# Turning half of a softmax tile through memory and VectorE squares instead of on TensorE, for three of sixteen attention units per image

## The reference

```python
# layer 0: group norm, 8 heads of 64 channels, projection, group norm, residual
hn = group_norm(x, gn1_scale, gn1_bias)
q, k, v = split(einsum('bchw,oc->bohw', hn, w_qkv) + b_qkv)      # per head, 64 x 1024 each
wgt = softmax(einsum('bct,bcs->bts', q * scale, k * scale))      # per head, 1024 x 1024
a = einsum('bts,bcs->bct', wgt, v)
x = x + group_norm(einsum('bchw,oc->bohw', a, w_proj) + b_proj, gn2_scale, gn2_bias)
# layer 1: one head of 512 channels, weights normalised, rms over q, k and v
scores = einsum('bci,bcj->bij', q1, k1) * 512 ** -0.5
h = einsum('oc,bcn->bon', w_out, einsum('bij,bcj->bci', softmax(scores), v1))
out = (x + h) * 2 ** -0.5
```

## Time and profile before

| | |
|---|---|
| median of 3 runs | 3375.08 us (3374.36 to 3375.76) |
| the profiled execution, its own time | 3375.88 us |
| its span, first to last instruction | 3373.7 us |
| TensorE busy | 3351.2 us, 99% |
| VectorE busy | 2132.7 us, 63% |
| ScalarE busy | 1838.7 us, 55% |
| GpSimd busy | 1064.3 us, 32% |
| granted TensorE clock | 1.00 of 2.4 GHz |
| DMA, mean | 98 GB/s |

### The profile page before, as it was taken

One profiled execution on the slowest core, in us unless ns is written; L12 is line 12 of the kernel. 1 busy time (PEld: TensorE's weight loads), 2 busy tenths in 40 slices (PEclk: granted clock), 3 DMA queues, 4 the chain that ended last, 5 costly groups with the idle time before them and its releaser, 6 DMA issues.

```text
span 3373.7 us, 51950 instructions
## 1 busy us (share of the span) xinstructions
PE 3351.2 (99%) x16816; PEld 2777.5 (82%) x16816; DVE 2132.7 (63%) x3489; ACT 1838.7 (55%) x3094; POOL 1064.3 (32%) x947
## 2 busy tenths in 40 slices
PE   8999999999999999999999999999999999999999
PEld 6888888888888888888888888888888888888887
DVE  5677357773578745786457854578555784557844
ACT  4677227862378523784337842388333882347822
POOL 1344104441045410453104531145211452124511
PEclk9999999999999999999999999999999999999999
DMA  8522244313534125331253212442224422343212
GB/s 340 149 67 59 79 131 124 93 34 94 140 99 101 62 57 151 103 86 76 53 167 91 73 75 76 144 101 63 93 61 144 98 63 94 92 139 70 63 57 75
DMA packets 109871, 332.15 MB, mean 98 GB/s; under 512 B 21760, under 2 KB 54784, under 8 KB 98816
## 3 DMA queue, kind: packets, MB, share of 16 engines
q1 hardware_dynamic: 107648, 322.15, 33.3%
q10 hardware_dynamic: 1920, 6.29, 0.9%
HBM read 162.68 MB, written 31.49 MB: 58 GB/s over the span
## 4 chain that ended last, share of the span: by engine, by line
PE 94%; DMA 2%; issue 1%; DVE 1%; SPq 1%; ACT 1%; POOL 0%; POOLq 0%; DVEq 0%
PE big L514 25%; PE big L648 14%; PE ops L634 14%; PE tps L619 14%; PE big L746 7%; PE big L655 5%; PE tps L819 5%; PE ops L819 5%; PE ops L598 3%; DMA ST<-ST 2%; PE tps L746 1%; SPq L419 0%; PE ops L746 0%; SPq L484 0%; PE ops L788 0%
## 5 line engine op out<-in xcount | busy, mean ns | idle before, releaser
L1097 POOL TENSOR_SCALAR PB<-PB,small 128x1024 f32<-128x1024 f32 x576 | 648.7, 1127 | 1294.8 <-DVE small L1342 1277.2
L1347 DVE TENSOR_TENSOR PT<-tps,PT 128x512 fp32r<-128x512 f32 x1024 | 652.5, 679 | 42.1 <-ACT PT L954 41.7
L1336 DVE TENSOR_REDUCE small<-big 128x1 f32<-128x1024 f32 x512 | 625.2, 1221 | 85.1 <-PE big L648 81.8
L954 ACT ACTIVATE PT<-tps 128x512 fp32r<-128x512 f32 x1024 | 564.1, 597 | 158.3 <-PE tps L619 155.4
L948 ACT ACTIVATE PB<-big,small 128x1024 f32<-128x1024 f32 x512 | 572.8, 1119 | 94.8 <-DVE small L1336 91.8
L634 PE MATMUL ops<-PT,VT 128*128 128x512 f32 x2048 | 599.1, 414 | 0.0
L648 PE MATMUL big<-ST 128*128 128x512 f32 x2048 | 554.2, 392 | 3.5 <-DMA ST<-ST 3.5
L619 PEld LDWEIGHTS tps<-ident,PB 128*128 128x128 f32 x4096 | 470.2, 140 | 95.4 <-DVE PT L1347 30.9
L619 PE MATMUL tps<-ident,PB 128*128 128x128 f32 x4096 | 545.7, 274 | 0.9
L648 PEld LDWEIGHTS big<-ST 128*128 128x128 f32 x2048 | 382.6, 188 | 91.5 <-issue 6.1
L634 PEld LDWEIGHTS ops<-PT,VT 128*128 128x128 f32 x2048 | 346.1, 189 | 47.1 <-DVE PT L1347 5.0
(11 more groups left out here) (188 smaller groups left out, 4911.7 us busy)
## 6 DMA issues: line engine op xcount, KB each, us to landing
ST<-ST SPq DMA_DIRECT2D x360, 256.0 KB, 5.3
W<-d_qk SPq DMA_DIRECT2D x32, 1024.0 KB, 7.0
W<-PB SPq DMA_DIRECT2D x256, 128.0 KB, 2.4
X<-in_x SPq DMA_DIRECT2D x8, 2048.0 KB, 10.2
W<-d_wp SPq DMA_DIRECT2D x8, 2048.0 KB, 11.9
W<-d_g SPq DMA_DIRECT2D x8, 2048.0 KB, 11.8
W<-d_m SPq DMA_DIRECT2D x8, 2048.0 KB, 7.7
W<-d_u SPq DMA_DIRECT2D x8, 2048.0 KB, 13.2
```

The costliest lines, as they stand in the source:

```text
L954: act_fn(pt_slot(u, s)[:, 0, :], tps[n % 2][:], ACT.Copy).then_inc(s_pt_hi, 1)
L1097: nc.gpsimd.tensor_scalar(PB[:, i, :], PB[:, i, :], rinv[:, i:i + 1], 1.0, ALU.mult, ALU.mult)\
L1336: V.tensor_reduce(negmax[:, i:i + 1], tile(("s", 4 * u + tb))[:], axis=AX.X, op=ALU.max, negate=True).then_inc(s_row_max, 1)
L1347: V.tensor_tensor(pt_slot(u, s)[:, 1, :], tps[n % 2][:], pt_slot(u, s)[:, 0, :].bitcast(f32), ALU.subtract).then_inc(s_pt_ready, 1)
```

## The change

It touches the first unit of pairs 0, 1 and 2 (units 0, 4 and 8, `MOVED`), and of these the slots 4 to 7, the second half of the keys.

- TensorE no longer turns these 4 slots. As each of the unit's 4 row blocks is normalised, its second half (128 x 512, 256 KB) is written to DRAM (`d_e`), the partitions split as 4 quarters of 32; once the four are there, 4 transfers of 256 KB bring them back to `X[:, 0:2, :]` (`F0`), 32 partitions each, in runs of 128 elements (`move_quarters`, on SyncE's queue).
- VectorE transposes 32x32 squares (`square`), one instruction per slot: slots 4 and 5 at the head of step 7 (ahead of `qk_lo` and `row_max`), slots 6 and 7 in step 9. ScalarE and VectorE then make the two parts from SBUF (`moved_hi`, `moved_lo`). `values0` of slots 4 and 5 moves from step 8 to step 9, of slots 6 and 7 from step 9 to step 10, ahead of the transposes.
- For the square to come out right the second half of the keys of pairs 0 to 2 is stored in another order (`keys_by_turn`): key 128 s + 32 q + r at column 128 q + 4 r + s. The query-key parts are written in that order, one tile in four. All four units of these pairs have it, so the transposes that stay on TensorE for slots 4 to 7 of units 4p+1 to 4p+3 read their stationary operand with a step of 4 elements, 16 bytes.
- Query-key tiles stand in steps 5, 7, 8 and 10.
- `X` is used as room, so the residual is loaded after pair 3's first stack, and scaled in steps 50, 52, 54 and 56.
- ScalarE waits for the writes to DRAM before it overwrites the row blocks (two units later); `corr(u, 0)` of a moved unit comes one step later.

```diff
-QK_STEPS = (5, 7, 9, 11)
+QK_STEPS = (5, 7, 8, 10)
...
+MOVED = [4 * pair for pair in range(PAIRS - 1)]
+MOVED_SLOTS = [8 * u + s for u in MOVED for s in range(4, NT)]
...
+SQUARES_FIRST, SQUARES_LAST = {7: (4, 5)}, {9: (6, 7)}
+MOVED_LO = {7: (4, 5), 9: (6, 7)}
+MOVED_VALUES = {9: (4, 5), 10: (6, 7)}
...
-X_SCALE_STEPS = (20, 23, 26, 29)
+X_SCALE_STEPS = (50, 52, 54, 56)
...
+        def keys_by_turn(pair, half, row):
+
+            if half and 4 * pair in MOVED:
+                return row.rearrange("p (q r s) -> p s q r", q=QUARTERS, s=4)
+            return row.rearrange("p (s q r) -> p s q r", q=QUARTERS, s=4)
...
+            def move_quarters(b, u):
+
+                if u:
+                    sp.wait_ge(s_squared, squared_count(b, 8 * (u - 4) + NT - 1))
+                    own_wait(sp)
+                for t in range(KB):
+                    sp.wait_ge(s_p_norm, b * 72 + 4 * u + t + 1)
+                    own_wait(sp)
+                    sp.dma_start(d_e.ap().rearrange("p q t n -> q p t n")[:, :, t, :], PB[:, t, HALF:N]).then_inc(s_moved_out, 16)
+                sp.wait_ge(s_moved_out, (b * len(MOVED) + MOVED.index(u) + 1) * 16 * KB)
+                own_wait(sp)
+                for q in range(QUARTERS):
+                    sp.dma_start(F0[32 * q:32 * q + 32, :, :, :],
+                                 d_e[:, :, :, P * q:P * q + P])\
+                      .then_inc(s_moved, 16)
...
-                sp.dma_start(X[:], src_x(b)).then_inc(s_x_res, 16)
+                move_quarters(b, 0)
...
+                move_quarters(b, 4)
                 stack_head(b, 2, 0)
                 stack_head(b, 2, 1)
+                move_quarters(b, 8)
                 stack_head(b, 3, 0)
+                sp.wait_ge(s_pt_ready, b * 144 + MOVED_SLOTS[-1] + 1)
+                own_wait(sp)
+                sp.dma_start(X[:], src_x(b)).then_inc(s_x_res, 16)
...
+                        if s >= 4 and u // 4 * 4 in MOVED:
+                            keys = row[:, HALF:N].rearrange("p (k s) -> p s k", s=4)[:, s - 4, :]
+                        else:
+                            keys = row[:, P * s:P * s + P]
+                        last = nc.tensor.transpose(tps[n % 2][:, P * t:P * t + P], keys, ident[:])
...
+                def square(n):
+                    u, s = n // 8, n % 8
+                    if s == 4:
+                        dve.wait_ge(s_moved, (b * len(MOVED) + MOVED.index(u) + 1) * 16 * QUARTERS)
+                    V.transpose(squared(s).rearrange("p (t q r) -> p t q r", t=KB, q=QUARTERS),
+                                F0.rearrange("p q t (r s) -> p s t q r", s=4)[:, s - 4, :, :, :])\
+                     .then_inc(s_squared, 1)
+
+                def moved_lo(n):
+                    dve.wait_ge(s_moved_hi, squared_count(b, n))
+                    slot = pt_slot(n // 8, n % 8)
+                    V.tensor_tensor(slot[:, 1, :], squared(n % 8), slot[:, 0, :].bitcast(f32), ALU.subtract)\
+                     .then_inc(s_pt_ready, 1)
```

More of the change, by code:

```diff
@@ L46, in qk_part, with of_moved, transposed, valued @@
     return None
+MOVED = [4 * pair for pair in range(PAIRS - 1)]
+MOVED_SLOTS = [8 * u + s for u in MOVED for s in range(4, NT)]
+def of_moved(step, table):
+    unit = 4 * (step // 16)
+    return [8 * unit + s for s in table.get(step % 16, ())] if unit in MOVED else []
+def transposed(step):
+    n = 2 * (step - LAG)
+    return [m for m in (n, n + 1) if m >= 0 and m not in MOVED_SLOTS]
+def valued(step):
+    n = 2 * (step - LAG) - 2
+    return [m for m in (n, n + 1) if m >= 0 and m not in MOVED_SLOTS]
+SQUARES_FIRST, SQUARES_LAST = {7: (4, 5)}, {9: (6, 7)}
+MOVED_LO = {7: (4, 5), 9: (6, 7)}
+MOVED_VALUES = {9: (4, 5), 10: (6, 7)}
 def a_parts(step):
@@ L104, in build @@
         d_r = nc.dram_tensor("d_r", [N], f32)
+        d_e = nc.dram_tensor("d_e", [P // QUARTERS, QUARTERS, KB, HALF], f32)
         X = sb("X", [P, KB, N])
@@ L616, in transposes @@
                     if n >= 2:
-                        pe.wait_ge(s_pt_ready, b * 144 + n - 1)
+                        bank_read = n - 2 if n - 2 not in MOVED_SLOTS else n - 6
+                        pe.wait_ge(s_pt_ready, b * 144 + bank_read + 1)
                     for t in range(4):
-                        last = nc.tensor.transpose(tps[n % 2][:, P * t:P * t + P],
-                                                   PB[:, 4 * (u % 2) + t, P * s:P * s + P], ident[:])
+                        row = PB[:, 4 * (u % 2) + t, :]
+                        if s >= 4 and u // 4 * 4 in MOVED:
[3 more added lines that the diff above has]
+                        last = nc.tensor.transpose(tps[n % 2][:, P * t:P * t + P], keys, ident[:])
                     last.then_inc(s_t_full, 1)
@@ L694, in body @@
                         out_block(proj0, 0, 1, 0)
-                    if n >= 0:
-                        transposes(n // 8, n % 8)
-                        transposes(n // 8, n % 8 + 1)
-                    if n > 0:
-                        values0(n - 2)
-                        values0(n - 1)
+                    for m in of_moved(step, MOVED_VALUES):
+                        values0(m)
+                    for m in transposed(step):
+                        transposes(m // 8, m % 8)
+                    for m in valued(step):
+                        values0(m)
                 values0(8 * UNITS0 - 2)
@@ L990, in body @@
                         qk_hi(qk_part(step))
-                    if n >= 0:
-                        pt_hi(n // 8, n % 8)
-                        pt_hi(n // 8, n % 8 + 1)
-                    if tb == 2 and u >= 2:
+                    for m in of_moved(step, SQUARES_FIRST):
+                        moved_hi(m)
+                    for m in transposed(step):
+                        pt_hi(m // 8, m % 8)
+                    if tb == 2 and u >= 2 and u - 2 not in MOVED:
+                        corr(u - 2, 0)
+                    if tb == 3 and u - 2 in MOVED:
                         corr(u - 2, 0)
@@ L1001, in body @@
                         last_v_hi(last_values(step))
+                    for m in of_moved(step, SQUARES_LAST):
+                        moved_hi(m)
                     for part in a_parts(step):
@@ L1327, in qk_lo @@
                     cols = slice(HALF * half, HALF * half + HALF)
-                    V.scalar_tensor_tensor(unstacked(what, 1)[:, cols], tile(("qk", j))[:, 0:HALF],
-                                           (bq, bk)[what][:, pair:pair + 1],
-                                           unstacked(what, 0)[:, cols].bitcast(f32), ALU.add, ALU.subtract)\
-                     .then_inc(s_nat_ready, 1)
+                    to, of, hi = unstacked(what, 1)[:, cols], tile(("qk", j))[:, 0:HALF], unstacked(what, 0)[:, cols]
+                    if what:
+                        to, hi = keys_by_turn(pair, half, to), keys_by_turn(pair, half, hi)
+                        of = of.rearrange("p (s q r) -> p s q r", q=QUARTERS, s=4)
+                    V.scalar_tensor_tensor(to, of, (bq, bk)[what][:, pair:pair + 1], hi.bitcast(f32),
+                                           ALU.add, ALU.subtract).then_inc(s_nat_ready, 1)
                 def row_max(u, tb):
@@ L1355, in body @@
                     u, tb, n = step // 4, step % 4, 2 * (step - LAG)
+                    for m in of_moved(step, SQUARES_FIRST):
+                        square(m)
                     if qk_part(step) is not None:
@@ L1365, in body @@
                         recip((step - 1) // 4, (step - 1) % 4)
-                    if n >= 0:
-                        pt_lo(n // 8, n % 8)
-                        pt_lo(n // 8, n % 8 + 1)
+                    for m in of_moved(step, SQUARES_LAST):
+                        square(m)
+                    for m in of_moved(step, MOVED_LO):
+                        moved_lo(m)
+                    for m in transposed(step):
+                        pt_lo(m // 8, m % 8)
                     if last_values(step) == NT - 1:
```

33 lines of the change are left out of this document (29 added, 4 removed).

## The result

The changed kernel takes 3585.04 us (median of 5 runs, 3582.24 to 3585.93), the kernel before 3375.51 beside it: ratio 1.0619, 95% interval 1.0604 to 1.0633. It is 6.2% slower, 209.5 us, far above the predicted range.

What follows compares the result with a forecast made beforehand. TensorE, busy 99% and 94% of the last chain, was taken as the bound. 3375.9 us - 20.9 (net gain of the move) + 4 (strided accesses) = 3359 us; range 3346 to 3412, likeliest case 3347 to 3366.

Steps and rivals of the forecast that it cites:

- The transfers: Stores and loads before step 7's squares: 7.3 to 9.4 us against 9.2 or 10.8 allowed, so no cost.
- The store is not as fast as the row: Rival, chance 0.28: the moved blocks' stores run on 4 of 16 engines and land late; 3366 to 3404 us.
- The wait before step 9's scores: TensorE waits for the query-key tile's buffer: 1.74 us from scores to scores, 0.83 us standing per pair.
- Removed transposes: TensorE, steps 7 to 10: transposes of 0.79 and 0.91 us go, fewer changes gain 0.2; 1.90 us per pair.
- VectorE in step 9: Its 4.9 us of work start late; slots 10 to 13 wait 0.45 us in all; cost 0.2 per pair.
- The strided accesses: VectorE's squares and the query-key writes with a step of 16 bytes cost little: +4 us in all.
- The slower rival: Chance 0.20: the remaining transposes' stepped weight loads cost some 50 ns each, 58 us in all; 3417 us.
- The rule on engines: A SyncE transfer uses the most engines up to 16 dividing both sides' outermost counts, here 4; the store rival's basis, 0.28.

Runs made afterwards that it cites:

- e1: The changed kernel with the DRAM buffer laid out [block, partition, key], so that stores have 128 as outermost count: 3392.93 us, ratio 1.0051.
- e12: e5 with DRAM laid out as 4 parts of 32 rows plus one padding row, the store 4 by 32 by 512: 3537.01 us, ratio 1.0477.
- e13: e5 with the four blocks interleaved in DRAM, the store 128 rows lying 8 KB apart, outermost dimension 128: 3376.37 us, ratio 1.0005.
- e11: The changed kernel with unused matmuls filling TensorE's gap after step 7's values, 32 in each image's first pair, otherwise 20: 3542.0 us, ratio 1.0495.
- e6: The kernel before with query-key tiles in steps 5, 7, 8 and 10 and nothing else: 3371.89 us, ratio 0.9984.
- e7: e2 without any 16-byte step, the order of keys, weights and squares as in e5: 3364.65 us, ratio 0.9966.
- e2: The changed kernel without its 8 transfers per unit, the squares turning whatever stands in X: 3391.94 us, ratio 1.0044.
- e3: The kernel before with the new key order alone, its stepped writes and weight reads in all 12 units of three pairs, nothing moved: 3408.43 us, ratio 1.0095.
- e9: e5 with the DRAM side of the stores written as 4 by 32 by 512, same bytes to the same addresses: 3367.98 us, ratio 0.998.
- e10: e5 with the DRAM side of the stores written as 8 by 16 by 512: 3369.03 us, ratio 0.9979.
- e5: The changed kernel with row-wise stores and no 16-byte steps, GpSimd writing moved halves in runs of 32 keys into X: 3369.35 us, ratio 0.998.

## Why the prediction was wrong

The step that failed is the one called **The transfers**, which ended with "I take no cost". It took the landing of a row store (2.4 us) for a store of another shape. The rival *The store is not as fast as the row* named the mechanism, four of sixteen engines, and e1, e12 and e13 show it; but it priced it at 11 to 49 us, and it measured 192 (after minus e1). Three of its terms were mis-sized:

- Stores run at 75 GB/s, not at a quarter of 430, 107. A store holds its engines 3.5 us (worked out from the rate), not 2.5, and all four queue up: the last lands 8.2 us after its block, not 5.2 to 5.8.
- The loads start on SyncE only then, and take 7.7 us with four issues (0.65 us each, one after another) where I had taken 4.7 to 6.8. 16.1 us in all against a deadline of 10.8: 5.3 late, close to the 5.45 us that TensorE waits.
- The clock was not in any sum. After the wait it is 0.50, which makes the next tile 2.1 us longer, 50 us in all (tiles of the changed kernel against those of e11).

**The wait before step 9's scores**: predicted 1.74 us from scores to scores and present in all 24 pairs, measured 1.72. This step was right, and so was its reading from the earlier trace rows. It has a tail that I left out: 0.13 and 0.09 us in the scores and the tile that follow.

**Removed transposes**: 1.90 us was right against step 8 of the kernel before, which has a late slot. Against e6, where a tile in step 8 takes that lateness away, it is 1.6, and 0.3 at the boundaries between values and transposes, so 1.9 again.

**VectorE in step 9, "Cost 0.2"**: too small. In e7 the groups of steps 10 to 13 of pair 1 take 0.8 us more than undisturbed ones, in e6 0.2; the wait that grew is that of the transposes for `pt_lo` (46.7 us in all on the weight loads, 23.2 in e6). I had VectorE level again from step 12; step 13 still waits. So the move brings 11.8 us (e7) where the working has 20.9.

**The strided accesses, "+4"**: e2 minus e7 is 27 us for all steps together. Some 13 of it are the weight loads (below), which leaves 14 for the squares and the writes, where the sum had 4. Squares read with a step cost 1.08 us, against 0.68 (e7) for the same squares in runs of 32, so the nearest row was no guide to a step of 16 bytes; the stepped writes cost 0.35 to 0.5 more. The upper bound, 12.5 for both, left out what follows them: scores that wait for a stack, 6 us more in e3. (With these 12.5 the range's upper end is 3367.5 and not 3366, and the range of the store rival, 3366 to 3404, leaves out the +4 of the sum.)

**The slower rival, weight loads with a step of 16 bytes**: right in kind, wrong in size. The record grows by 71 ns, the pace by 11 ns per transpose, below the 15 from which it decides. 1152 x 11 ns = 13 us, not 58. The statement "nothing hides it" was what failed: 60 of the 71 ns don't show in the pace. The Trainium skill, "SBUF — State Buffer", section "Door 1: The DMA port swizzle", has each new 16-byte line pay a penalty. The duration of the load agrees with that (211 ns against 140), the pace hardly.

**The rule on engines**: the Trainium skill, "DMA: Bandwidth & Descriptors", section "Why a DMA increments its semaphore by 16 and not by 1", has the number of engines follow from the outermost counts of both sides. The trace agrees: a count of 4 gives a share of 0.23 to 0.27 and 12 packets fewer per store, one of 128 gives up to 0.9. That the count in the source isn't always what decides is shown by e9 and e10, written with 4 and 8 and run like 128. I gave this rule a chance of 0.28, though the argument against it ("loads may be quicker than assumed") did not speak to it at all.

How the 209.5 us add up, each term between two runs: the move with its tile steps -12 (e7 minus before); the 16-byte steps +27 (e2 minus e7); transfers over 16 engines +1 (e1 minus e2); late transfers through four engines +149 (e11 minus e1) and +43 (after minus e11), 192 in all, of which the clock is about 50 and the waiting the rest. The sum is 208; the kernel before itself differs by 1 us between the chips. GpSimd's second operation is no part of the change; with the transfers it is 5 us (e5 minus e7), at the edge of what can be told.

## What to carry to other kernels

A transfer's outermost dimension belongs beside its size: of the two that were measured, 4 and 128, 128 is the one to write, and the DMA share of a window while the transfer runs tells which it became (0.25 went with four engines), as does the count of small packets. The landing time is no help: the page has none for these stores in the two slow kernels. Where a transfer feeds an engine whose next work sits in front of the bound engine's buffer release, lateness goes through undiminished, and TensorE's low clock adds to it. The permutation was cheaper here where the data are written anyway in runs of 32 (GpSimd's normalising, 0.2 to 0.3 us more per block) than as a step of 16 bytes on every reader and writer.

## What the runs showed of the hardware that was not expected

- Stepped weights (16 bytes) lengthen the recorded load of 128 columns from 140 to 211 ns, and the distance between transposes by only 11 ns.
- VectorE's 32x32 transposes of 128x512 take 1.08 us when read with a step of 16 bytes and 0.68 in runs of 32.
- A store over four engines has 12 packets fewer than one over sixteen (171008 against 172160 for 96 stores), so the count of packets tells the engines where no landing time is given.
- Matmuls whose results nobody uses made the kernel 43 us faster: they kept the granted clock at 1.00 through a wait that was no shorter (173.2 us in all against 166.9).
- GpSimd's scaling of 128x1024 takes 1.13 to 1.16 us as one operation and 2 x 0.69 as two of half the width.
